# One accumulator for the expert rows, gated rows, and a copy moved from VectorE to ScalarE

## The reference

```
scores = sigmoid(h @ w_router)                  # 2048 tokens x 32 experts
topk_idx = 6 experts of the best 4 of 8 groups  # by scores + corr_bias
routed = sum over the 6 experts of scores[e] * (silu(h @ gate_w[e]) * (h @ up_w[e])) @ down_w[e]
shared = (silu(h @ sh_gate_w) * (h @ sh_up_w)) @ sh_down_w
out = x1 + gb * (routed + shared)               # x1: after attention; gb: one row per batch
```

## Time and profile before

| what | value |
|---|---|
| median of three runs | 536.52 us |
| the profiled execution | 533.56 us |
| its span, first to last instruction | 531.8 us |
| mean granted clock of PE | 0.938 |
| busy: PE, VectorE, ScalarE, GpSimd | 457.2, 224.8, 176.1, 287.7 us |
| indirect scatters in the loop | 104 |
| indirect row scatters of `dispatch` | 96 |

### The profile page before, as it was taken

How to read it: one execution, slowest core, us unless ns; L and a number is a source line. 1 busy time by engine, 2 the same in 40 slices (tenths; PEclk the granted TensorE clock), 3 DMA queues, 4 the chain that set the end, 5 groups by cost and what they waited for, 6 DMA issues and landing times.

```text
span 531.8 us, 9471 instructions
## 1 busy us (share of the span) xinstructions
PE 457.2 (86%) x1994; PEld 318.3 (60%) x1995; DVE 224.8 (42%) x971; ACT 176.1 (33%) x429; POOL 287.7 (54%) x257
## 2 busy tenths in 40 slices
PE   4899879798799999349999999999999999999600
PEld 4355656447447655327777777777777777776400
DVE  1934687727875551013333333333333333333202
ACT  2232231222231322104444444444444444444300
POOL 1500711576877777704565556566666556656530
PEclk9999897899898999859999999999999999999955
DMA  8999411133458899535677575666656567666388
GB/s 279 339 334 366 180 41 40 63 129 118 166 146 284 284 302 357 202 89 97 99 117 110 95 119 89 108 114 113 103 98 117 96 104 115 114 97 104 41 247 246
DMA packets 86193, 83.25 MB, mean 157 GB/s; under 512 B 22329, under 2 KB 80155, under 8 KB 86172
## 3 DMA queue, kind: packets, MB, share of 16 engines
q1 hardware_dynamic: 63708, 50.49, 33.3%
q0 software_dynamic: 20160, 30.43, 30.1%
q10 hardware_dynamic: 2304, 2.10, 1.2%
HBM read 43.13 MB, written 40.90 MB: 158 GB/s over the span
## 4 chain that ended last, share of the span: by engine, by line
PE 79%; DMA 7%; DVE 5%; issue 3%; ACT 2%; POOL 2%; SPq 1%; POOLq 0%; ACTq 0%
PE bank L1446 23%; PE bank L1461 17%; PE bank L1363 8%; PE bank L1263 6%; PE bank L1439 5%; PE bank L1454 4%; PE bank L1374 4%; PE bank L1249 3%; DMA gate_up<-token_sums 2%; PE bank L1165 2%; PE bank L1336 2%; DMA token_sums<-tok_buf,dest 2%; DMA XH<-in_L_attn_x 1%; PE bank L1197 1%; PE bank L1301 1%
## 5 line engine op out<-in xcount | busy, mean ns | idle before, releaser
L588 POOL DMA_INDIRECT token_sums<-tok_buf,dest x104 | 161.4, 1552 | 118.7 <-ACT tok_buf L778 51.4
L1446 PE MATMUL bank<-gate_up,tok_buf 128*128 x416 | 141.3, 462 | 0.4 <-DVE tok_buf L1112 0.4
L1112 DVE COPY tok_buf<-bank 128x256 f32<-128x256 f32 x104 | 44.1, 424 | 187.3 <-PE bank L1439 185.4
L560 POOL DMA_INDIRECT pair_rows<-XH,rows_i x96 | 94.9, 989 | 44.3 <-issue 28.4
L1461 PE MATMUL bank<-down,tok_buf 88*128 x416 | 109.0, 384 | 0.0
L1446 PEld LDWEIGHTS bank<-gate_up,tok_buf 128*128 128x128 f32 x416 | 79.4, 191 | 29.1 <-issue 1.7
L1461 PEld LDWEIGHTS bank<-down,tok_buf 88*128 88x128 f32 x416 | 70.6, 190 | 7.6 <-issue 0.2
L778 ACT ACTIVATE tok_buf<-bank,tok_buf 128x256 f32<-128x256 f32 x104 | 49.2, 473 | 53.2 <-PE bank L1461 52.6
L763 ACT ACTIVATE tok_buf<-bank 128x176 f32<-128x176 f32 x104 | 33.0, 317 | 91.2 <-PE bank L1446 91.2
L1439 PEld LDWEIGHTS bank<-ident,tok_buf 128*128 128x128 f32 x208 | 27.4, 142 | 48.5 <-issue 24.0
L1439 PE MATMUL bank<-ident,tok_buf 128*128 128x128 f32 x208 | 41.2, 280 | 17.6 <-DMA tok_buf<-pair_rows 14.6
(11 more groups left out here) (153 smaller groups left out, 433.5 us busy)
## 6 DMA issues: line engine op xcount, KB each, us to landing
tok_buf<-pair_rows SPq DMA_DIRECT2D x104, 128.0 KB
gate_up<-in_L_ffn_gate_w SPq DMA_DIRECT2D x8, 704.0 KB, 8.2
gate_up<-in_L_ffn_up_w SPq DMA_DIRECT2D x8, 704.0 KB, 9.0
down<-in_L_ffn_down_w SPq DMA_DIRECT2D x2, 2816.0 KB
pair_rows<-sh_rows SPq DMA_DIRECT2D x1, 5120.0 KB, 18.9
XH<-in_L_attn_x SPq DMA_DIRECT2D x4, 512.0 KB, 10.1
token_sums<-sh_rows ACTq DMA_DIRECT2D x16, 128.0 KB, 6.2
gate_up<-token_sums SPq DMA_DIRECT2D x4, 512.0 KB, 5.4
```

The source lines that it names most:

```text
L560: nc.gpsimd.indirect_dma_start(out=pair_rows, out_offset=bass.IndirectOffsetOnAxis(ap=rows_i[:, t, k:k + 1], axis=0), in_=XH[:, t, :], in_ ...
L588: nc.gpsimd.indirect_dma_start(out=token_sums[c % 2], out_offset=bass.IndirectOffsetOnAxis(ap=dest[:, c:c + 1], axis=0), in_=yw[:, c, :], ...
L1112: V.tensor_copy(xT[:, c % 2], banks[0][:, 0:C].rearrange("p (k n) -> p k n", k=KC)).then_inc(xT_copied, 1)
L1446: last = mm(banks[1 + c % 2][:, 0:M2], xT[:, c % 2, k, :], gate_up[:, bass.ds(e * (KC * M2) + k * M2, M2)], start=k == 0, stop=k == KC - 1)
```

## The change

The output tensor itself is the accumulator. x1 is stored into `out` as it is; the shared expert's down weights are multiplied by gb (by batch 0's for its tokens; a copy for batch 1 goes to HBM and comes back later), its rows go by accumulating DMAs from GpSimd's queue into `out`; the routed rows are multiplied by the pair's weight and by the gate row of their token's batch before they are scattered into `out`. For this each record carries two more columns that flag the token's batch, ScalarE makes the first batch's part of the gate row (`gate_of_first`), VectorE adds the second's (`make_gate`) and `weigh`, now on VectorE, multiplies by both. `copy_x` goes to ScalarE. The reciprocal, `divide` and the last stage are gone. Scatter n waits for the three before it, unless a flag in the map, loaded on GpSimd per block, says that the block isn't the first of its expert. `blocks(..., apart=2)` writes out two turns on GpSimd ahead of its loop.

```diff
-        token_sums = [nc.dram_tensor(f"token_sums{a}", (T, C), f32).ap() for a in range(2)]
+        gated_down = nc.dram_tensor("gated_shared_down", (SM, C), f32).ap()
+        tokens_out = out.rearrange("b n c -> (b n) c")
...
+        homes = [XH_flat[:, a * HOME:a * HOME + GT * C].rearrange("p (i c) -> p i c", c=C) for a in range(NT // GT - 1)]
+        row_gate = [XH_flat[:, a * HOME + GT * C:(a + 1) * HOME] for a in range(2)]
...
         @program.sync
-                    sp.wait_ge(divided, n + 1)
-                    sp.dma_start(rows_g, shares[b][g]).then_inc(shares_stored[n], 16)
+                    await_read(sp, ("proj", b, (g + 1) * GT - 2))
+                    await_read(sp, ("proj", b, (g + 1) * GT - 1))
+                    sp.dma_start(out_v[:, b, g * GT:(g + 1) * GT, :], X[:, n * GT:(n + 1) * GT, :]).then_inc(x1_stored[n], 16)
...
+            await_computed(sp, ("sd", 0, TB - 1))
+            for m, (a, n) in enumerate(SC):
+                sp.dma_start(sh_dn[0:n, m, :], gated_down[a:a + n, :]).then_inc(gated_back, 16)
             sp.wait_ge(recs_ready, 2 * B)
...
         @program.gpsimd
+            def gate_shared_down():
+                pool.wait_ge(heads_clear, 16)
+                pool.wait_ge(gb_ready, B)
+                pool.wait_ge(ld_sh, 16 * (2 + len(SC)))
+                link(nc.gpsimd.tensor_copy(gates[:, :, :], gb))
+                for m, (a, n) in enumerate(SC):
+                    last = nc.gpsimd.tensor_tensor(second_down[0:n, m, :], sh_dn[0:n, m, :], gates[0:n, 1, :], ALU.mult)
+                link(last)
+                for m, (a, n) in enumerate(SC):
+                    last = nc.gpsimd.tensor_tensor(sh_dn[0:n, m, :], sh_dn[0:n, m, :], gates[0:n, 0, :], ALU.mult)
+                last.then_inc(down_gated, 1)
+            def add_shared(g, home):
+                pool.wait_ge(shared_ready, (g + 1) * GT)
+                pool.wait_ge(x1_stored[g], 16)
+                nc.gpsimd.dma_start(out_v[:, g // NG, g % NG * GT:(g % NG + 1) * GT, :], homes[home],
+                                    accum_op=ALU.add).then_inc(shared_added[g], 16)
...
-            dispatch(32, NT * TOPK)
+            dispatch(32, 60)
+            add_shared(0, 0)
+            dispatch(60, NT * TOPK)
+            for g in range(1, NT // GT):
+                add_shared(g, g % (NT // GT - 1))
...
+            for g in range(NT // GT):
+                pool.wait_ge(shared_added[g], 16)
+            def scatter(c, n, base, fresh):
+                for j in range(1, min(n, R - 1) + 1 if isinstance(n, int) else R):
+                    count = base if c >= j else base - 16
+                    pool.wait_ge(scattered[(c - j) % R], count if isinstance(count, int) else count - 16 + fresh)
                 pool.wait_ge(y_scaled, n + 1)
                 pool.wait_ge(dest_ready, n + 1)
-                wait(pool, scattered[(c - 2) % R], 16 * turns)
...
             def step(turn, last):
+                fresh = [pool.value_load(map_i[0:1, bass.ds(2 * MAP_W + R * turn + c, 1)], min_val=0, max_val=16)
+                         for c in range(R + last)]
...
         @program.scalar
+            def gate_of_first(c, turn, n):
+                act_e.wait_ge(rec_loaded[c], 16 * turn + 16)
+                if not isinstance(n, int) or n >= 2:
+                    act_e.wait_ge(y_scaled, n - 1)
+                nc.scalar.activation(row_gate[c % 2], gates[:, 0, :], ACT.Copy,
+                                     scale=rec[:, c, E + 1:E + 2]).then_inc(first_gate, 1)
...
                     if not last or c + 1 < R:
                         silu(c + 1, n + 1)
+                    if not last or c + 2 < R:
+                        copy_x(c, n + 2)
                     copy_act(c, n)
-                    if not first(n):
-                        weigh((c - 1) % R, n - 1)
+                    gate_of_first(c, turn, n)
...
         @program.vector
             def second_norm(b, g):
+                dve.wait_ge(x1_stored[b * NG + g], 16)
...
+            def make_gate(c, n):
+                dve.wait_ge(first_gate, n + 1)
+                V.scalar_tensor_tensor(out=row_gate[c % 2], in0=gates[:, 1, :], scalar=rec[:, c, E + 2:E + 3], in1=row_gate[c % 2],
+                                       op0=ALU.mult, op1=ALU.add).then_inc(gate_made, 1)
+            def weigh(c, turn, n):
+                dve.wait_ge(y_done, n + 1)
+                dve.wait_ge(weight_ready, n + 1)
+                dve.wait_ge(gate_made, n + 1)
+                if not first(turn):
+                    dve.wait_ge(scattered[c], 16 * turn)
+                V.scalar_tensor_tensor(out=yw[:, c, :], in0=banks[4 + c % 2][:, 0:C], scalar=pair_weight[:, c:c + 1],
+                                       in1=row_gate[c % 2], op0=ALU.mult, op1=ALU.mult).then_inc(y_scaled, 1)
...
-                    if not last or c + 2 < R:
-                        copy_x(c, n + 2)
+                    if not first(n):
+                        make_gate((c - 1) % R, n - 1)
                     if not last or c + 1 < R:
                         multiply(c + 1, n + 1)
                     if not first(n):
+                        weigh((c - 1) % R, turn if c > 0 else turn - 1, n - 1)
                         bound_tokens((c - 1) % R, n - 1)
                     pick_weight(c, turn, n)
```

More of the change, by code:

```diff
@@ L370, in load_values, with blocks @@
                 map_i[0:1, bass.ds(section * MAP_W + 1 + first + R * turn, 2 * R)], engines=(which,),
-                min_val=0, max_val=(E - 1, (T - P) * PITCH + E - 1)[section],
+                min_val=0, max_val=(E - 1, (T - P) * PITCH + E - 1, 16)[section],
                 skip_runtime_bounds_check_because="the map's entries are clamped where they are made")
             return values
-        def blocks(eng, step):
+        def blocks(eng, step, apart=1):
             last_turn = load_last_turn(eng)
-            step(0, False)
-            with eng.Fori(1, FEWEST) as turn:
+            for turn in range(apart):
+                step(turn, False)
+            with eng.Fori(apart, FEWEST) as turn:
                 step(turn, False)
@@ L593, in step @@
             def step(turn, last):
+                fresh = [pool.value_load(map_i[0:1, bass.ds(2 * MAP_W + R * turn + c, 1)], min_val=0, max_val=16)
+                         for c in range(R + last)]
                 for c in range(R):
                     n = R * turn + c
[L597 to L598 removed]
+                    if c > 0:
+                        scatter(c - 1, n - 1, 16 * turn + 16, fresh[c])
+                    elif not first(n):
+                        scatter(R - 1, n - 1, 16 * turn, fresh[c])
                     if last and c == R - 1:
[L600 to L609 removed]
+                        scatter(c, n, 16 * turn + 16, fresh[c + 1])
+            blocks(pool, step, 2)
         @program.scalar
@@ L788, in step @@
                         silu(c + 1, n + 1)
+                    if not last or c + 2 < R:
+                        copy_x(c, n + 2)
                     copy_act(c, n)
-                    if not first(n):
-                        weigh((c - 1) % R, n - 1)
-                    if last and c == R - 1:
-                        weigh(c, n)
+                    gate_of_first(c, turn, n)
             blocks(act_e, step)
@@ L1147, in step @@
                     if last and c == R - 1:
+                        make_gate(c, n)
+                        weigh(c, turn, n)
                         bound_tokens(c, n)
             blocks(dve, step)
-            dve.wait_ge(gb_back, 16)
-            for g in range(NT // OT):
-                rows_g = slice(g * OT, (g + 1) * OT)
-                total = sums[:, 0, rows_g, :]
-                dve.wait_ge(summed[g], 16)
-                V.tensor_tensor(total, total, over(gb_again[:, g * OT // TB, :], [P, OT, C], 1), ALU.mult).then_inc(out_ready, 1)
         @program.tensor
```

160 lines of the change are left out of this document (59 added, 101 removed).

## The result

The changed kernel takes 547.64 us, median of 4 runs (546.79 to 549.38), beside 536.58 for the kernel before: ratio 1.0209, 95% interval [1.0182, 1.0236]. It is slower, as forecast, and lies in the range; but it is slower by 11 us where 23 were forecast (559.4). Two terms of the sum were far off, in opposite directions.

A forecast was written before the change was run, and what follows sets the result against it. PE was taken to bound the loop before the change. First scatter at 241.9, loop 308.3 and end 4.5 gave a 554.7 us span, plus 1.76 and 2.96 for 559.4; forecast 541 to 575, cases 529 to 592.

The forecast's parts named there:

- The tail goes: After the last scatter: only 3.9 us landing and 0.6 us semaphores remain of 26.5 us, winning 22.0 us.
- The order of the scatters: Block loop: 22 full waits, 15 at expert changes and 7 in written-out turns, at 5.2 us each.
- The flags: GpSimd's queue: four flag loads a turn add 2.0 us, making 22 gaps of 3.85 us at turn starts.
- rival 2: Flag loads: GpSimd's queue doesn't run ahead, turn gap 5.05 us, +26.4, 585.8 us; chance 0.24.
- rival 1: Flag loads entirely hidden by the queue and full waits at 4.6 us: loop 279.4, 530.0 us; chance 0.14.
- Before the loop: Ahead of the first scatter: reciprocal saves 3.25 us, one accumulating DMA adds 1.5; first scatter at 241.9 against 243.09.
- GpSimd is late, not the data: Loop start: first rows come some 1.7 us earlier, so GpSimd sets the first scatter, at 241.9 us.
- the prediction's last paragraph: Signs to check: a first scatter after 245 us would mean the three accumulates land later under the loop's first row loads.
- rival 3: Loop: GpSimd's descriptor work stands still during make_gate, 104 times 0.48 us, +50, 609 us; chance 0.03.
- VectorE and ScalarE in the loop: Block loop: VectorE needs 1.8 us of 2.5 a block, ScalarE about 1.55; neither becomes the bound.

The follow-up runs named there:

- the combined kernel: Changed kernel with one load per turn's flags, flags from the first block, earlier gating of shared weights, three accumulating transfers behind the first gathers: 524.85 us, 0.9803.
- the copy alone: Kernel before with only copy_x moved from VectorE to ScalarE, after silu: 535.58 us, 0.9994.

## Why the prediction was right in direction and wrong in size

**The tail goes: right, 3.7 us short.** The 26.5 us became 8.2. What failed is "3.9 us to land and some 0.6": the landing took 2.72, and after it GpSimd's drain went on for 5.2 us. The ten other traces of kernels with this end show the same, the span ending 5.3 to 5.7 us after the last landing (the combined kernel: 515.41 and 520.8). The trace of the kernel before has such a drain too, which the prediction didn't read. It began at 514.1 and ended at 531.6, 4.5 us after GpSimd's last accumulating transfer had landed (VectorE's multiply that needed it starts at 527.12); there the last multiply and store filled that time. What a drain waits for is not shown.

```profile
L55 POOLq DRAIN  x1: 17466/17466/17466, 514.1 to 514.1; - x1
```

**The order of the scatters: the count nearly right, the price a little high.** 21 full waits at 4.91, not 22 at 5.2: block 7 is scattered in the third turn and uses the flag, and the 21 landings that were awaited took 3.86 us in the mean, with 1.05 from landing to start. All 15 changes of expert stand where the inputs put them.

**The flags: the step that failed.** This term was mis-sized most: 3.85 us for the gap at a turn's start, measured 2.91, or 1.06 more than the plain gap instead of 2.0. The load that I priced was one of 506 ns with 190 of check; in the loop it takes 289 and 147. And I put one price on every turn, where the timeline shows two. Eight of the 23 gaps are 3.40 to 3.99 us, about as priced: in each of them GpSimd had waited, for landings or for VectorE, at the block before or at the one before that (480.92 behind 476.93, 493.23 behind 487.98), so that its queue had no lead: the first of the four loads began from 0.47 us before to 0.12 us after the start of the scatter ahead of the gap. Fourteen are 1.85 to 2.83, in the mean 2.16: there the loads began 0.80 to 2.67 us before that start, and cost 0.3 us. The last one, 6.55 at block 99 (523.78), stands where the loop is left for the last turn; it is not the flags' alone, since the gap there is 4.90 in the trace of the kernel before. PE, forecast well under 95% busy in the loop, was at 95.9%. So rival 2 (never ahead) is out, and rival 1 (hidden entirely) too, since taking the loads together saves 5 us of the loop. The truth lies between, nearer to rival 1 than I put it. The Trainium skill, page "Runtime: NRT & Kernel Launch", section "Instruction fetch mechanics", gives about 200 ns a register: the 289 ns are nearer to it than to the 506 that decided, though the 0.55 us with its checks is not.

**Before the loop: the claim "GpSimd is late, not the data" failed, by 12.4 us.** The sum let the three transfers land undisturbed and the loads run beside them undisturbed; the prediction's last paragraph names this as what a first scatter after 245 would mean, but the sum did not price it. From the end of the dispatch on, the first scatter came 7.5 us later than summed, and leaving the transfers out gives 8 us back. Another 2.1 us are a later start of the dispatch, 96.67 instead of 97.81 - 3.25. That is the gating, and moving it gives 2.6 back: its 5.7 us were called covered by GpSimd's idle time, but they stood beside VectorE's work, which was on the path. The remaining 2.8 us are the length of the dispatch, 133.25 us instead of 128.93 + 1.5. They are no price of the change that the runs show: with the copy alone, where the dispatch is the one of the kernel before, it took 133.15 as well. The Trainium skill, page "SBUF — State Buffer", section "Who interferes with whom", has just this pair exclude each other: here the traces agree, 0.22 against 0.76 us. For the scatters I read the rule as not biting, from a pick_weight that started inside a scatter. In the median that held, 1551 ns with make_gate beside them. But the eight scatters that started under a running make_gate did wait for it: rival 3's mechanism is real, and it cost 1.1 us in all instead of 50.

**The two errors hide each other.** The loop was 25 us too dear and its start 12 us too cheap. With the loop alone put right, the forecast would have been 534.5, no slower than before. So the right direction was in part luck: the full waits were nearly right, but without the loop's excess the sum would not have come out slower, because it lacked the 12 us of the start. Using the flags from the first block on, which takes away the six waits of the written-out turns, brings the kernel level with the one before (536.56).

**VectorE and ScalarE in the loop: right.** Neither became the bound: of 230 us of the loop they are busy for 121.90 and 110.79. The 1.8 us a block for VectorE don't follow from their own terms, which give 1.45 (82.81 / 91 - 0.42 + 2 x 0.48); measured are 1.42. The copy alone is 0.9994; weigh and make_gate on VectorE were not tried alone.

## What to carry to other kernels

A wait on every transfer of a chain is priced at the landing plus the issue, and it is paid again at each start-up turn that is written out with plain counts; count those too. Work put into an engine's idle time is free only if it takes nothing from what is busy in that time, a neighbour's operand reads or the transfers that others wait for; look at what else runs there. A cost that is hidden where a queue has a lead is paid in full where it has none: price the two kinds of place apart, and count them.

## What the runs showed of the hardware

- A register load on SP's queue of eight values takes 1.86 us in the median, 3.58 to 3.59 with one accumulating transfer beside it (two traces) and 6.00 to 6.81 with three (six traces).
- On GpSimd's queue four values cost 0.33 us in one load and 4 x 0.29 in four.
- A scatter that starts while make_gate runs on VectorE, with two inputs in SBUF and 0.17 to 0.36 us left, takes 0.05 to 0.24 us longer than 1.55 (eight of 104); the 63 within which make_gate starts took 1.59 us at most.
- The 96 row scatters of the dispatch took 128.93 us in the trace of the kernel before and 133.15 in that of the copy alone, with the same dispatch code.
- GpSimd's drain at the program's end goes on 5.2 us after its last scatter has landed, and the span ends with it.
- With four transfers of 128 numbers, 4 bytes a partition, just ahead of it, a row store took 16.9 us to land instead of 3; with 16 numbers each and 40 us earlier it took its usual time. Which of the two mattered was not tried apart.
- PE's granted clock is 0.50, the lower of its two levels (1.2 of 2.4 GHz), from 230 to 244 us, where it is busy for 0.88 us, and 0.63 over the whole stretch up to 256. In the combined kernel, where it is busy for 24.45 of these 26 us, it is 0.89.
